# The second bias of the dense experts: one product of gates and biases for all token blocks, in place of a selector product per expert and block

## The chip, the core and the metric

The kernel runs on one core of one Trainium2 chip, in one launch. The metric is the device time of that core in microseconds (us). TensorE (PE) multiplies matrices, VectorE (DVE), ScalarE (ACT) and GpSimd (POOL) do the elementwise work, and SyncE (SP) issues the transfers. Each engine takes its own instructions in order and waits on semaphores for the others.

## What is computed

A two-layer language-model tower over 16 x 256 = 4096 tokens of width 256. Layer 0 has a time mix and a channel mix, then a mixture of 8 dense experts of width 1024. Layer 1 has a recurrence, attention with 16 heads, and 4 further experts. The change touches the 8 dense experts alone:

```python
logits = xf @ Wr + br                               # [tokens, 8]
weights = softmax(where(logits >= 2nd largest, logits, -inf))
h = gelu(einsum('td,edh->eth', xf, W1) + b1[:, None, :])
expert_out = einsum('eth,ehd->etd', h, W2) + b2[:, None, :]
out = einsum('etd,te->td', expert_out, weights)
```

`b2` is the second bias, one row of 256 numbers per expert. Its share of `out` is `weights @ b2`, a product of [4096 x 8] and [8 x 256].

## The kernel before, in words

The tokens are split into 8 blocks (TILES) of 512, each of 4 sub-blocks (SUB) of 128 tokens. `phase_a` (to about 520 us) makes layer 0 up to the input of the experts, for all blocks; the residual `c.h` stays in on-chip memory as fp32. `phase_bc` then runs passes. Pass i (0 to 7) takes the 8 dense experts of block i; from pass 1 on the layer-1 work of block i - 1 ("front": recurrence, attention, router) is woven in, and from pass 2 on the layer-1 experts of block i - 2 as well. Passes 3 to 6 are one loop. Two more passes hold the rest of layer 1. **Pass 0** (about 520 to 726 us) has dense work alone, and brings in and splits all weights (`low` on DVE, `high` on ACT). Passes 1 and 7 have dense and front work; passes 2 to 6 all three kinds.

All products are of bf16 parts: a fp32 number is a high and a low bf16 part, and a product takes three matmuls (high x high, low weight x high, high weight x low).

A pass of dense work is made of 64 units U0 to U63 ("up", 6 matmuls of 512 columns into one of two banks `c_up`) and 64 units D0 to D63 ("down", 12 matmuls of 256 columns into the two banks `c_down`). D8e to D8e+7 belong to expert e. ACT makes gelu of each U twice (fp32 `c_g` and bf16 `c_hi`), POOL makes the low part `c_lo`. D waits for both. After an expert's last D, DVE (`taken`, L1910) adds gate x `c_down` to `c.h`: four instructions.

In what order the units stand among the front's steps is written down in ORDER_F, which `Plan.braid` mixes with the plan's units by estimated costs; ORDER_0 is pass 0. Every engine goes through the same list and does its own part of each entry. In passes 2 to 6 the list near the dense units named later reads (front's steps by name, experts' units left out):

- `f1 U2 f1x U3 D0 U4 f2`: f1 transposes the normed input (L2004), f1x splits it (ACT, then POOL's `c_xlo`), f2 multiplies it (L1973).
- `Zx0 A1 U13 D8 D9 Z0 Rx1 ...`: the recurrence (A, R, Z steps), mostly DVE.
- `f5d U20 D16 D17 g5 U21 D18 f6`: f5d and g5 norm again (DVE, POOL), f6 transposes (L2004).
- `D24`, `D32`: among the heads of the first sequence (Sa, Sb score on PE, E the exponentials on ACT).
- `m3 D40 m4 D41 m5`: row maxima of the second sequence (PE scores into four banks, DVE reduces).
- `G20 D48 Sa6 E6`: among its heads, next to a gated expert unit.
- `g13 b0 U61 D56 D57 D58 U62 y0 D59 b1`: b0 and y0 norm (DVE, POOL), b1 transposes (L2004).

The bias before: `c.b2s` holds the three bf16 parts of `b2` for 8 experts in 24 of 128 rows, and `c.sel[:, e, :]` is a matrix of zeros with ones in the three rows of expert e. At the first D of an expert (D0, D8, ..., D56), each of the 4 sub-blocks starts with one matmul `c.sel[:, e, :] x c.b2s` (L2234), which puts the expert's bias row into every token's accumulator; the gate is applied later with the rest. These are 4 matmuls per expert and block, called "the selector group of D8e" below: 4 x 8 x 8 = 256.

Of the kernel before, what the change touches and what calls it, by code (L numbers as in the profile page):

```python
# [8 lines left out]
ALU = mybir.AluOpType  # L9
# [115 lines left out]
def phase_a(nc, c):  # L125
# [6 lines left out]
    with ExitStack() as x:  # L132
# [81 lines left out]
        def _(sp):  # L214
# [11 lines left out]
            for j in range(3):  # L226
                sp.wait_ge(s_p, 9 + 2 * j)
                sp.dma_start(c.b2s[j:3 * E0:3, :], c.b2p[:, j, :]).then_inc(s_b2, 16)
# [6 lines left out]
            sp.wait_ge(s_b2, 3 * 16)  # L235
# [739 lines left out]
def phase_bc(nc, c, out):  # L975


    KF, KE, KR = 109, 17, TILES * SUB + 5 + 13 + 2 * sum(kind != "B" for kind, _ in FIRST_LOADS)
    PB = GROUP
    VW = HD + 1  # L980
    with ExitStack() as x:
# [81 lines left out]
        w0 = mix0[:, :, :].rearrange("p s e -> p (s e)")  # L1063
        spare = lo14[:, 0:4, :].rearrange("p k n -> p (k n)").bitcast(F32)
# [35 lines left out]
        stored = count("stored", 16)  # L1100

# [71 lines left out]
        def run(eng, start, splits, dense, front, gates):  # L1173
# [3 lines left out]
            go(ORDER_0, splits, dense(0, PLAN_B, None))  # L1177
# [136 lines left out]
        def _(pool):  # L1314
# [69 lines left out]
            run(pool, lambda: None, {}, dense, front, lambda t: {})  # L1384

        @block.scalar
        def _(act):
# [163 lines left out]
            run(act, start, {"x%d" % u: lambda a=a: high(*a) for u, a in SPLITS.items()}, dense, front, gates)  # L1551

        @block.vector
        def _(dve):
# [407 lines left out]
            run(dve, start, {"x%d" % u: lambda a=a: low(*a) for u, a in SPLITS.items()}, dense, front, gates)  # L1962

        @block.tensor
        def _(pe):
# [220 lines left out]
            def dense(i, plan, before):  # L2186
# [37 lines left out]
                def down(u):  # L2224
# [78 lines left out]
            run(pe, lambda: None, {}, dense, front, lambda t: {})  # L2303
# [99 lines left out]
```

## Time and profile before

| | |
|---|---|
| times of three runs | 3225.17, 3230.91, 3234.37 us; median 3230.91 us |
| profiled execution | 3222.42 us, its span 3220.4 us |
| mean granted clock of TensorE | 0.959 of full speed |
| PE, ACT, DVE, POOL busy | 86%, 55%, 53%, 44% of the span |

The span is what the trace covers; 2.0 us of the execution lie around it. PE is the busiest engine, and what it waits for is spread thinly over the passes: how much a removed matmul is worth depends on what PE waits for next. In rows of the trace a matmul's duration includes the part in which it overlaps the next one, so the distance from one start to the next tells what one costs in a stream.

### The profile page before, as it was taken

The page shows a single profiled execution, that of the slowest core. Times are in us where ns is not written, and L with a number is a line of the kernel's source. Part 1 is how long each engine was busy: PE and PEld are TensorE (multiplying, and loading weights), DVE is VectorE, ACT ScalarE, POOL GpSimd, SP SyncE. Part 2 cuts the span into 40 slices and gives each one's busy share as a digit, 9 for nine tenths or more (in the row PEclk, how much of TensorE's full clock was granted, in tenths as well). Part 3 has the DMA queues.
Part 4 walks back from the last instruction along what each step waited for, and adds up shares of the span by engine and source line. Part 5 has one row for each costly group of instructions (what it writes and reads, how often), then busy time and mean ns, then how long its engine had stood idle before and what let it go on. Part 6 is the DMA issues. An engine that isn't in the chain of part 4 may idle for free. (4 is left out here: it accounts for less than half of the span.)

```text
span 3220.4 us, 58240 instructions
## 1 busy us (share of the span) xinstructions
PE 2778.5 (86%) x21884; PEld 1859.2 (58%) x22208; DVE 1695.8 (53%) x3163; ACT 1785.4 (55%) x2819; POOL 1407.7 (44%) x1326
## 2 busy tenths in 40 slices
PE   3787866898899999999999999999999998987778
PEld 1454544565665566566655665566656665663555
DVE  6777754636444635463446344635464446446552
ACT  2444534555665566656655665566556655664634
POOL 5454522443445444544454444444544343453334
PEclk8898987999999999999999999999999999999999
DMA  2000004842112122222222222222222222110002
GB/s 67 14 13 26 13 14 165 322 171 71 66 67 78 69 71 76 91 73 72 72 91 70 72 76 80 81 71 76 79 83 71 70 73 73 53 53 27 24 22 74
DMA packets 59721, 235.94 MB, mean 73 GB/s; under 512 B 6560, under 2 KB 25024, under 8 KB 40640
## 3 DMA queue, kind: packets, MB, share of 16 engines
q1 hardware_dynamic: 57920, 228.13, 20.3%
q0 software_dynamic: 1536, 4.20, 0.5%
q8 instruction: 176, 2.88, 0.4%
q14 instruction: 89, 0.73, 0.1%
HBM read 200.57 MB, written 31.72 MB: 72 GB/s over the span
## 5 line engine op out<-in xcount | busy, mean ns | idle before, releaser
L1381 POOL TENSOR_TENSOR c_lo<-c_g,c_hi 128x512 bf16<-128x512 f32 x720 | 888.2, 1241 | 1341.8 <-ACT c_hi L1543 1216.9
L2220 PE MATMUL c_up<-c_xT,c_ring 128*128 128x512 bf16 x2855 | 707.4, 384 | 78.4 <-ACT c_hi L1543 52.4
L2237 PE MATMUL c_down<-c_ring,c_hi 128*128 128x256 bf16 x4096 | 714.7, 275 | 0.0
L1542 ACT ACTIVATE c_g<-c_up,b 128x512 f32<-128x512 f32 x512 | 353.2, 690 | 491.5 <-PE c_up L2220 487.7
L2237 PE MATMUL c_down<-c_ring,c_lo 128*128 128x256 bf16 x2048 | 563.2, 275 | 0.0
L2220 PEld LDWEIGHTS c_up<-c_xT,c_ring 128*128 128x128 bf16 x3072 | 294.7, 99 | 362.3 <-ACT c_hi L1543 64.1
L2237 PEld LDWEIGHTS c_down<-c_ring,c_hi 128*128 128x128 bf16 x4096 | 397.4, 98 | 106.2 <-issue 1.7
L1543 ACT ACTIVATE c_hi<-c_up,b 128x512 bf16<-128x512 f32 x512 | 351.1, 686 | 0.0
L1809 DVE CAST c_room<-c_room 128x384 bf16<-128x384 f32 x256 | 127.1, 528 | 403.2 <-PE c_front L2132 307.8
L1542 ACT ACTIVATE c_g<-c_up 128x512 f32<-128x512 f32 x176 | 105.5, 600 | 291.7 <-PE c_up L1973 285.6
L2237 PEld LDWEIGHTS c_down<-c_ring,c_lo 128*128 128x128 bf16 x2048 | 201.5, 98 | 25.4
L1359 POOL TENSOR_TENSOR c_room<-c_room 128x384 bf16<-128x384 f32 x176 | 169.6, 977 | 61.4 <-DVE c_room L1809 61.4
L1973 PE MATMUL c_up<-c_hi,c_ring 128*128 128x512 bf16 x674 | 171.8, 388 | 19.7 <-ACT c_hi L1543 14.3
L2293 PE MATMUL c_down<-c_ring,c_hi 128*128 128x192 bf16 x1024 | 143.2, 258 | 25.0 <-DVE h L1910 25.0
L1973 PE MATMUL c_up<-c_yhi,c_ring 128*128 128x512 bf16 x476 | 131.4, 397 | 38.6 <-ACT c_hi L1543 26.2
L1910 DVE SCALAR_TENSOR_TENSOR h<-c_down,c_gates,h 128x256 f32<-128x256 f32 (+1 forms) x256 | 106.0, 475 | 81.9 <-PE c_down L2237 81.4
L1498 ACT ACTIVATE c_room<-c_front 128x384 f32<-128x384 f32 x256 | 115.7, 489 | 51.6 <-PE c_front L2108 47.4
L1784 DVE TENSOR_REDUCE c_mx<-c_front 128x2 f32<-128x512 f32 (+1 forms) x192 | 117.8, 682 | 47.4 <-PE c_front L2083 41.5
L1542 ACT ACT_TABLE_LOAD x101 | 129.6, 1283 | 10.9 <-PE c_up L2220 9.3
L2104 PE MATMUL c_front<-c_room,c_kz 128*128 128x256 bf16 (+1 forms) x512 | 120.0, 247 | 18.0 <-ACT c_room L1498 18.0
L2293 PE MATMUL c_down<-c_ring,c_lo 128*128 128x192 bf16 x512 | 132.0, 258 | 0.0
L1973 PEld LDWEIGHTS c_up<-c_hi,c_ring 128*128 128x128 bf16 x712 | 68.4, 99 | 90.6 <-issue 18.7
(334 smaller groups left out, 5439.2 us busy)
## 6 DMA issues: line engine op xcount, KB each, us to landing
c_ring<-kept_dense SPq DMA_DIRECT2D x112, 1024.0 KB, 4.8
c_ring<-kept_experts SPq DMA_DIRECT2D x63, 512.0 KB, 3.3
c_room<-in_WB SPq DMA_DIRECT2D x16, 1024.0 KB, 7.1
kept_dense<-c_ring SPq DMA_DIRECT2D x16, 1024.0 KB, 4.8
c_ring<-kept_experts SPq DMA_DIRECT2D x28, 384.0 KB, 3.4
kept_experts<-c_room SPq DMA_DIRECT2D x9, 512.0 KB, 4.1
c_xT<-kept_xT SPq DMA_DIRECT2D x8, 512.0 KB, 4.7
out<-h SPq DMA_DIRECT2D x8, 512.0 KB, 6.5
```

Source lines behind the costliest of these rows:

```text
L1359: pool.tensor_tensor(pl[:, n % PB, :], pf[:, n % PB, :], ph[:, n % PB, :], ALU.subtract).then_inc(p_lo_pool.sem, 1)
L1381: pool.tensor_tensor(lo14[:, a, :], g[:, h % 4, :], hi14[:, a, :], ALU.subtract).then_inc(lo_ready.sem, 1)
L1498: act.activation(pf[:, n % PB, :], fb[n % 2][:, 0:3 * P], ACT.Exp).then_inc(p_f.sem, 1)
L1542: act.activation(g[:, h % 4, :], ub[n % 2][:, :], ACT.Gelu, bias=bias)
L1543: act.activation(hi14[:, a, :], ub[n % 2][:, :], ACT.Gelu, bias=bias).then_inc(hi_ready.sem, 1)
L1784: dve.tensor_reduce(o, fb[n % 4][:, :].rearrange("p (h k) -> p h k", k=w), AX.X, ALU.max).then_inc(mx_ready.sem, 1)
L1809: dve.tensor_copy(ph[:, n % PB, :], pf[:, n % PB, :]).then_inc(p_hi.sem, 1)
L1973: m = pe.matmul(bank[:, :], w(wp, k, e * P, P), xs[xp][:, k, :], start=(j == 0 and k == 0), stop=(j == 2 and k == kc - 1))
L2104: pe.matmul(bank[:, lo:lo + w], kz[h % 2][:, h // 2, ks_:ks_ + P], qT[:, h // 2, qs_:SEQ], start=True, stop=False, skip_group_check=True)
L2220: last = pe.matmul(ub[n % 2][:, :], r[:, wp, o + q * P:o + (q + 1) * P], xT[:, xp, q, :], start=(m == 0 and q == 0), stop=(m == 2 and q == ...
L2237: m = pe.matmul(bank, (hi14, lo14)[xp][:, a, s * P:(s + 1) * P], r[:, wp, o + KC * P:o + CHUNK], start=False, stop=(k == HC0 - 1 and n == ...
L2293: m = pe.matmul(ob[s // 2][:, (s % 2) * D:(s % 2) * D + DZ], (hi14, lo14)[xp][:, a, s * P:(s + 1) * P], E(plan, wp, name, k, 0, DZ), start ...
```

## The change

The bias part is computed once for all 4096 tokens, in the second half of pass 0.

- DVE (`gate_parts`) clears 128 columns per sub-block in `lo14` (name `c_lo`), splits the fp32 gates into three bf16 parts, and writes six column groups of 8: BIAS lists which part of the gate meets which part of the bias (six of the nine pairs). `c.b2s` gets six groups of 8 rows to match (six small DMAs in place of three).
- PE transposes these 32 tiles of 128 x 128 in four rounds (gT0 to gT3) into the front's banks; ACT copies each round of 1024 columns to `hi14` (name `c_hi`).
- PE then makes 16 products of a pair of sub-blocks (`bias0` to `bias15`, two matmuls of 256 columns each), and DVE adds each (128 x 512) to `c.h`.
- ORDER_0 places them: gate parts behind D43, gT0 to gT3 behind D44 to D47, bias0 to bias15 behind D48 to D63.
- The 256 selector matmuls go. The first product of the group (L2280 in the changed kernel) starts the accumulation.

```diff
+BIAS = ((0, 0), (0, 1), (1, 0), (0, 2), (2, 0), (1, 1))
...
-            for j in range(3):
+            for m, (_, j) in sorted(enumerate(BIAS), key=lambda q: q[1][1]):
                 sp.wait_ge(s_p, 9 + 2 * j)
-                sp.dma_start(c.b2s[j:3 * E0:3, :], c.b2p[:, j, :]).then_inc(s_b2, 16)
+                sp.dma_start(c.b2s[m * E0:(m + 1) * E0, :], c.b2p[:, j, :]).then_inc(s_b2, 16)
...
+        bias = ["gparts"] + ["gT%d" % r for r in range(4)] + ["bias%d" % q for q in range(TILES * SUB // 2)]
         for u in PLAN_B.units:
             if u[0] == "U":
                 ORDER_0.append("x%d" % u[1])
             ORDER_0.append(u)
+            if u[0] == "D" and u[1] >= NB - len(bias):
+                ORDER_0.append(bias[u[1] - NB + len(bias)])
...
+            def transposed_gates(r):                      # ACT
+                def f():
+                    act.wait_ge(gT_ps.sem, r + 1)
+                    act.activation(gT[:, r * 8 * P:(r + 1) * 8 * P], fb[r][:, :].bitcast(BF16),
+                                   ACT.Copy).then_inc(gT_ready.sem, 1)
...
+            def gate_parts():                             # DVE
+                part = [gparts[:, :, m * E0:(m + 1) * E0] for m in range(len(BIAS))]
+                low_of = sl[:, 0:TILES * SUB * E0].rearrange("p (s e) -> p s e", e=E0)
+                R.done(dve.memset(lo14[:, 0:8, :], 0.0))
+                R.done(dve.tensor_copy(part[0], mix0[:, :, :]))
+                R.done(dve.tensor_tensor(low_of, mix0[:, :, :], part[0], ALU.subtract))
+                R.done(dve.tensor_copy(part[1], part[0]))
+                R.done(dve.tensor_copy(part[3], part[0]))
+                R.done(dve.tensor_copy(part[2], low_of))
+                R.done(dve.tensor_tensor(low_of, low_of, part[2], ALU.subtract))
+                R.done(dve.tensor_copy(part[5], part[2]))
+                R.done(dve.tensor_copy(part[4], low_of))
+            def bias(q):
+                def f():
+                    dve.wait_ge(bias_ps.sem, q + 1)
+                    at = slice(q * TT, (q + 1) * TT)
+                    dve.tensor_tensor(c.h[:, at], c.h[:, at], fb[q % 4][:, :], ALU.add).then_inc(bias_used.sem, 1)
...
-                            pe.matmul(bank, c.sel[:, e, :], c.b2s[:, :], start=(s % 2 == 0), stop=False,
-                                      skip_group_check=True)
                         for n, (wp, xp) in enumerate(PARTS):
                             m = pe.matmul(bank, (hi14, lo14)[xp][:, a, s * P:(s + 1) * P],
-                                          r[:, wp, o + KC * P:o + CHUNK], start=False, stop=(k == HC0 - 1 and n == 2),
+                                          r[:, wp, o + KC * P:o + CHUNK], start=(k == 0 and n == 0 and s % 2 == 0),
+                                          stop=(k == HC0 - 1 and n == 2),
...
+            def transposed_gates(r):                      # PE
+                def f():
+                    if r == 0:
+                        pe.wait_ge(r_steps.sem, r_steps.at(0, KR))
+                    for j in range(8):
+                        m = pe.transpose(fb[r][:, :].bitcast(BF16)[:, j * P:(j + 1) * P], gparts[:, 8 * r + j, :],
+                                         c.identb[:, :])
+                    m.then_inc(gT_ps.sem, 1)
+            def bias(q):
+                def f():
+                    pe.wait_ge(gT_ready.sem, q // 4 + 1 if q > 3 else 4)
+                    if q >= 4:
+                        pe.wait_ge(bias_used.sem, q - 3)
+                    for j in range(2):
+                        s = 2 * q + j
+                        m = pe.matmul(fb[q % 4][:, j * D:(j + 1) * D], gT[:, s * P:(s + 1) * P], c.b2s[:, :],
+                                      start=(j == 0), stop=True, skip_group_check=True)
+                    m.then_inc(bias_ps.sem, 1)
```

(In `gate_parts` the waits between dependent steps are left out here.)

PE's rows at the first D of the fifth expert of pass 0 (D40), before the change (buffer numbers shown, `c_down0` and `c_down1` are the two accumulators):

```order
L2220 MATMUL c_up0<-c_xT,c_ring3 128x512 x6
L2234 MATMUL c_down0<-b2s,sel 128x256
L2237 MATMUL c_down0<-c_ring2,c_hi14 128x256 x2
L2237 MATMUL c_down0<-c_ring2,c_lo14 128x256
L2234 MATMUL c_down0<-b2s,sel 128x256
L2237 MATMUL c_down0<-c_ring2,c_hi14 128x256 x2
L2237 MATMUL c_down0<-c_ring2,c_lo14 128x256
L2234 MATMUL c_down1<-b2s,sel 128x256
```

The L2234 rows go from every such place, and the rest stays in its order. PE's rows in pass 0 from the last quarter of D44 on, in the changed kernel (L2352 are the transposes of gT0, L2265 an up unit):

```order
L2280 MATMUL c_down1<-c_ring3,c_hi14 128x256 x2
L2280 MATMUL c_down1<-c_ring3,c_lo14 128x256
L2352 MATMUL c_front0<-identb,c_lo14 128x128 x8
L2265 MATMUL c_up0<-c_xT,c_ring0 128x512 x6
L2280 MATMUL c_down0<-c_ring3,c_hi14 128x256 x2
```

Eight transposes now stand between D44 and U48, and so on for three more units; behind each of the last sixteen D units stand two matmuls of 256 columns. DVE's rows in pass 0 around D43, in the changed kernel (L1613 is a split of arriving weights, L1983 to L1996 are the gate parts):

```order
L1926 SCALAR_TENSOR_TENSOR h<-c_down1,c_gates,h 128x256 x2
L1613 TENSOR_TENSOR c_ring1<-c_room0,c_ring1 128x1024 x2
L1983 MEMSET c_lo14 128x2048
L1985 CAST c_lo14<-c_gates 128x32x8
L1987 TENSOR_TENSOR c_sl<-c_gates,c_lo14 128x256
L1988 COPY c_lo14<-c_lo14 128x32x8
L1989 COPY c_lo14<-c_lo14 128x32x8
L1991 CAST c_lo14<-c_sl 128x32x8
L1993 TENSOR_TENSOR c_sl<-c_sl,c_lo14 128x256
```

The gate parts stand between the split of the weights that U52 to U55 use (L1613, `c_ring1`) and the next split, at U48's place in the list. Nothing else moves, but what stands behind them on DVE waits for them.

## Rows read from the trace of the kernel before

**Rows 1.** The page's busy time of each engine.

```profile
PE 2778.5 (86%) x21884; PEld 1859.2 (58%) x22208; DVE 1695.8 (53%) x3163; ACT 1785.4 (55%) x2819; POOL 1407.7 (44%) x1326
```

**Rows 2.** Groups by line and shape: busy us, mean ns; idle before, releasers.

```profile
L2234 PE MATMUL c_down<-b2s,sel 128*128 128x256 bf16 x256 | 71.2, 278 | 10.3 <-DVE h L1910 9.1 <-issue 1.1
```

**Rows 3.** Timeline of PE at D0 of pass 4: start us, us.

```profile
1661.23 0.27 PE L2234 MATMUL c_down<-b2s,sel 128*128 128x256 bf16 x1
1661.34 0.38 PE L2237 MATMUL c_down<-c_ring,c_hi 128*128 128x256 bf16 x2
```

**Rows 4.** Chain that ended last, pass 7: start us, us, what.

```profile
2618.43 0.27 PE c_down L2234
...
2655.62 3.36 DVE c_room L1702
...
2753.46 0.12 PE c_down L2234
...
2825.02 0.11 PE c_down L2234
...
2858.29 0.11 PE c_down L2234
```

**Rows 5.** Timeline of POOL and PE behind D0 of pass 4.

```profile
1662.95 2.27 POOL L1349 TENSOR_TENSOR c_xlo<-c_room,c_xhi 128x512 bf16<-128x512 f32 x2
...
1665.28 0.60 PE L1973 MATMUL c_front<-c_xlo,c_WF 128*128 128x512 bf16 x2
```

**Rows 6.** Timeline of PE behind D8, D40 and D48 of pass 4.

```profile
1717.75 0.59 PE L2220 MATMUL c_up<-c_xT,c_ring 128*128 128x512 bf16 x2 [0.87 <-ACT c_hi L1543]
...
1874.80 0.22 PE L2083 MATMUL c_front<-mask,identb 128*128 128x128 bf16 x1
1875.11 0.28 PE L2081 MATMUL c_front<-c_kz,c_room 128*128 128x256 bf16 x1
...
1910.70 0.28 PE L2104 MATMUL c_front<-c_room,c_kz 128*128 128x256 bf16 x1 [1.34 <-ACT c_room L1498]
```

**Rows 7.** PE's waits in pass 3 (1343 to 1662): us in total, times, longest.

```profile
PE c_down L2293 <- DVE h L1910: 4.8, 1, 4.8
...
PE c_front L2004 <- DVE c_xn L1572: 0.2, 1, 0.2
```

**Rows 8.** Timeline of ACT behind D24 of pass 4.

```profile
1813.86 0.93 ACT L1498 ACTIVATE c_room<-c_front 128x384 f32<-128x384 f32 x2 [0.48 <-PE c_front L2108]
```

**Rows 9.** Timeline of DVE and PE behind D56 of pass 4.

```profile
1952.02 2.03 DVE L1572 TENSOR_SCALAR c_xn<-c_h,c_brs 128x256 f32<-128x256 f32 x4 [1.73 <-POOL c_brs L1328]
...
1954.33 0.93 PE L2004 MATMUL c_front<-ident,c_xn 128*128 128x128 f32 x7
```

**Rows 10.** Pass 0's last part: stretch, us, busy of PE, PEld, DVE, ACT, POOL, granted clock, DMA.

```profile
655.00:726.00 71.00, 70.58 (x498) 49.17 (x504) 15.63 (x22) 40.00 (x60) 30.05 (x26) 1.00 0.47 173
```

**Rows 11.** Nearest rows for the new work, groups and one timeline row.

```profile
L1625 DVE MEMSET c_kz<- 64x1024 uint32 x2 | 1.8, 912 | 0.5 <-issue 0.5
L1764 DVE CAST c_qs<-c_room 128x256 bf16<-128x256 f32 x32 | 9.4, 294 | 2.2
L1721 DVE TENSOR_TENSOR h<-h,c_front 128x512 f32 x8 | 5.1, 679 | 0.0
L1477 ACT ACTIVATE c_room<-c_front 128x1024 bf16<-128x1024 bf16 x32 | 32.7, 1021 | 9.4 <-PE c_front L2063 9.4
1767.40 0.62 PE L2063 MATMUL c_front<-identb,c_ks 128*128 128x128 bf16 x8 [0.60 <-DVE c_ks L1771]
```

**Rows 12.** Timeline of DVE in pass 0, the split for U48.

```profile
680.97 1.27 DVE L1597 TENSOR_TENSOR c_ring<-c_room,c_ring 128x1024 bf16<-128x1024 f32 x1 [7.49 <-ACT c_ring L1406]
```

**Rows 13.** Timeline of DVE and PE where pass 1 begins.

```profile
730.90 4.73 DVE L1572 TENSOR_SCALAR c_xn<-h,c_fmv,c_frs 128x256 f32<-128x256 f32 x4 [1.40 <-POOL c_frs L1328]
...
736.44 1.04 PE L2004 MATMUL c_front<-ident,c_xn 128*128 128x128 f32 x8
```

**Rows 14.** Pass 4 behind the longest wait, columns as in rows 10.

```profile
1695.00:1698.40 3.40, 3.35 (x22) 3.04 (x23) 3.40 (x3) 0.00 (x0) 0.00 (x0) 0.52 0.00 0
```

More of the change, by code:

```diff
@@ L975, in phase_bc @@
 def phase_bc(nc, c, out):
-    KF, KE, KR = 109, 17, TILES * SUB + 5 + 13 + 2 * sum(kind != "B" for kind, _ in FIRST_LOADS)
+    KF, KE, KR = 109, 17, TILES * SUB + 5 + 13 + 9 + 2 * sum(kind != "B" for kind, _ in FIRST_LOADS)
     PB = GROUP
@@ L1063, in phase_bc @@
         w0 = mix0[:, :, :].rearrange("p s e -> p (s e)")
+        gparts = lo14[:, 0:8, :].rearrange("p k n -> p (k n)").rearrange("p (s r) -> p s r", r=P)
+        gT = hi14[:, 0:8, :].rearrange("p k n -> p (k n)")
         spare = lo14[:, 0:4, :].rearrange("p k n -> p (k n)").bitcast(F32)
@@ L1100, in phase_bc @@
         stored = count("stored", 16)
+        gT_ps, gT_ready, bias_ps, bias_used = (count(n, 0) for n in ("gT_ps", "gT_ready", "bias_ps", "bias_used"))
         up_ps = Both(x.enter_context(nc.semaphore("c_up_ps")), NB, len(PLAN_C.bank_user))
@@ L1171, in go, with run @@
                         stage[o]()
-        def run(eng, start, splits, dense, front, gates):
+        def run(eng, start, splits, biases, dense, front, gates):
             start()
-            go(ORDER_0, splits, dense(0, PLAN_B, None))
+            go(ORDER_0, splits, dense(0, PLAN_B, None), biases)
             go(ORDER_B, dense(1, PLAN_B, PLAN_B), front(0))
@@ L1383, in dense @@
                 return tokens_of(i, plan, step)
-            run(pool, lambda: None, {}, dense, front, lambda t: {})
+            run(pool, lambda: None, {}, {}, dense, front, lambda t: {})
         @block.scalar
@@ L1550, in gates @@
                 return {"r2x": r2x}
-            run(act, start, {"x%d" % u: lambda a=a: high(*a) for u, a in SPLITS.items()}, dense, front, gates)
+            def transposed_gates(r):
[3 more added lines that the diff above has]
+                                   ACT.Copy).then_inc(gT_ready.sem, 1)
+                return f
+            run(act, start, {"x%d" % u: lambda a=a: high(*a) for u, a in SPLITS.items()},
+                {"gT%d" % r: transposed_gates(r) for r in range(4)}, dense, front, gates)
         @block.vector
@@ L1961, in gates @@
                 return {"r2": r2}
-            run(dve, start, {"x%d" % u: lambda a=a: low(*a) for u, a in SPLITS.items()}, dense, front, gates)
+            def gate_parts():
+                part = [gparts[:, :, m * E0:(m + 1) * E0] for m in range(len(BIAS))]
+                low_of = sl[:, 0:TILES * SUB * E0].rearrange("p (s e) -> p s e", e=E0)
+                R.done(dve.memset(lo14[:, 0:8, :], 0.0))
+                R.settle()
+                R.done(dve.tensor_copy(part[0], mix0[:, :, :]))
+                R.settle()
+                R.done(dve.tensor_tensor(low_of, mix0[:, :, :], part[0], ALU.subtract))
+                R.done(dve.tensor_copy(part[1], part[0]))
+                R.done(dve.tensor_copy(part[3], part[0]))
+                R.settle()
+                R.done(dve.tensor_copy(part[2], low_of))
+                R.settle()
+                R.done(dve.tensor_tensor(low_of, low_of, part[2], ALU.subtract))
+                R.done(dve.tensor_copy(part[5], part[2]))
+                R.settle()
+                R.done(dve.tensor_copy(part[4], low_of))
+                assert R.n == KR
+            def bias(q):
[3 more added lines that the diff above has]
+                    dve.tensor_tensor(c.h[:, at], c.h[:, at], fb[q % 4][:, :], ALU.add).then_inc(bias_used.sem, 1)
+                return f
+            run(dve, start, {"x%d" % u: lambda a=a: low(*a) for u, a in SPLITS.items()},
+                {"gparts": gate_parts, **{"bias%d" % q: bias(q) for q in range(TILES * SUB // 2)}},
+                dense, front, gates)
         @block.tensor
@@ L2302, in dense @@
                 return tokens_of(i, plan, step)
-            run(pe, lambda: None, {}, dense, front, lambda t: {})
+            def transposed_gates(r):
[6 more added lines that the diff above has]
+                    m.then_inc(gT_ps.sem, 1)
+                return f
+            def bias(q):
[8 more added lines that the diff above has]
+                    m.then_inc(bias_ps.sem, 1)
+                return f
+            run(pe, lambda: None, {}, {**{"gT%d" % r: transposed_gates(r) for r in range(4)},
+                                       **{"bias%d" % q: bias(q) for q in range(TILES * SUB // 2)}},
+                dense, front, lambda t: {})
 def program(nc, ins, out):
```

2 lines of the change are left out of this document (1 added, 1 removed).

## The prediction

> **What bounds the kernel now.** I first read the page's busy time: PE works for 2778.5 of 3220.4 us [rows 1], so at first sight every matmul that goes is a gain. The groups by shape give the removed ones: 256 selector matmuls, 278 ns each by their rows [rows 2]. That mean is not what they cost. In PE's timeline the selector starts at 1661.23 and the next matmul at 1661.34 [rows 3]: the rest of the 0.27 us overlaps. A 256-column matmul in a stream costs 0.11 us, a selector group of four 0.44 us, all 64 groups 28.2 us.
>
> Whether the 0.44 us reaches the end depends on what PE meets next. If its next wait ends at a time that the earlier part of PE's queue does not set, the wait grows by 0.44 us and nothing is gained. So I read the chain that ended last (which can be followed through pass 7), the list of PE's waits in pass 3, and the timelines of PE, ACT, DVE and POOL behind each group of pass 4, which is like passes 2 to 6.
>
> In pass 7 the chain runs through the groups of D0, D32, D48 and D56 [rows 4]. Not so at D8 and D16, where it is on DVE for the recurrence (the reciprocal of 3.36 us is one piece), nor at D24 and D40. Pass 1 has the same list and I take the same four.
>
> In passes 2 to 6, group by group:
> - D0: the low part of f2 starts at 1665.28, and POOL ends `c_xlo` at 1662.95 + 2.27 = 1665.22 [rows 5]. PE already waits there, for work that began with f1 and U2, ahead of D0. Lost.
> - D8: the next wait is 0.87 us, for a gelu that stands on ACT behind exponentials for the recurrence [rows 6]. Lost. D16: f6 waits 0.2 us for DVE's norm [rows 7]. Lost.
> - D24: PE's next wait is for a gelu behind the exponentials of a head, and these had idled 0.48 us for PE's score matmuls [rows 8]. PE sets the chain. Kept; D32 likewise, four heads on.
> - D40: between m3 and m4 the score matmuls wait for DVE to free a bank, 0.31 us from one start to the next at 1874.80 where 0.06 us is a 128-column one's pace [rows 6]. Lost. D48: the next score waits 1.34 us for ACT, which is behind the gated unit started before D48 [rows 6]. Lost.
> - D56: DVE ends the norm at 1952.02 + 2.03 = 1954.05, and PE starts b1 at 1954.33 [rows 9]. Less the 0.06 us that the hand-over took at D0 [rows 5], some 0.2 us of the 0.44 can be kept.
>
> **The change, part by part.** *Removed in passes 1 and 7:* 2 x 4 x 0.44 = 3.5 us. *In passes 2 to 6:* 5 x (0.44 + 0.44 + 0.2) = 5.4 us. *In pass 0:* from 655 to 726 us PE is busy for 70.58 of 71.00 us at full clock [rows 10], and the groups of D32 (just before it), D40, D48 and D56 count: 1.8 us. The first four stand before waits for arriving weights, seen in the timeline, and are lost. Together 10.7 us.
>
> *Added on PE, all in that full stretch of pass 0.* 16 x 2 products of 256 columns at 0.11 us: 3.5 us. 32 transposes: eight of the same shape take 0.62 us with the overlap of the last [rows 11]. Less that overlap it is about 0.06 us each, with it 0.08; I take 0.06, the pace of a 128-column matmul: 1.9 us. Together 5.4 us, and nothing covers them.
>
> The Trainium skill (TensorE: Matmul & The Clock Gate, section Back-to-back issue gap) gives about 81 ns for each matmul of 128 columns in a stream of weight loads and matmuls. By it the transposes would cost 2.6 us and the sum below would be 0.7 us less of a gain. The eight transposes of rows 11 speak for the smaller figure.
>
> *Added on DVE: the gate parts.* Memset of 2048 words: twice the 1024 of 0.91 us, 1.8 us. Six copies or casts of 256 columns at 0.29 us, 1.8 us. Two subtractions of 256 columns, each under the 0.68 us for 512 columns, say 0.4 us [rows 11]. With the waits between them 4.6 us. DVE had been idle for 7.49 us before the split at 680.97 [rows 12], so they run from 673.5 to 678.1. PE comes to gT0 when D44 ends: 19 D and 16 U units of 12 x 0.11 = 1.3 us and two selector groups ahead of 726.3, about 679.9, and 0.9 us earlier for the two groups gone, 679.0. No wait, with 0.9 us to spare. Should DVE's steps take twice as long beside POOL, they end at 682.7 and PE stands 3.7 us: that is the upper bound. Behind them the split for U56 to U59 comes at most that much later, and it is needed some 20 us on.
>
> *ACT's four copies* of 1024 columns cost 1.02 us each [rows 11], 4.1 us, in a stretch where ACT is busy for 40 of 71 us. A late gelu holds an up unit only if it is two units late, and a unit takes PE 3.1 us here: hidden. *DVE's 16 additions* cost 0.68 us each [rows 11], under 15.6 of 71 us busy: hidden but for the last. It stands ahead of the norm of pass 1. The norm ends at 730.90 + 4.73 = 735.63 and PE starts f1 at 736.44 [rows 13], 0.8 us to spare. The addition takes 0.7 of it, and PE is there 0.2 us earlier (0.44 less for D0, 0.22 more for bias15). f1 then waits about 0.2 us, and I take that off D0 of pass 1. *PE waits for DVE* to free one of four banks only four products back, over 10 us. *SP's three more DMAs* of 8 rows are issued before the first pass of layer 0 has anything for SP: nothing.
>
> **The sum.** 10.7 - 0.2 - 5.4 = 5.1 us less: 3222.4 - 5.1 = 3217.3 us for the profiled execution. The median of the runs shown is 8.5 us above that execution, so the median after is 3230.9 - 5.1 = 3225.8, say 3226 us. Of the 28 us of PE's work that go, 5.4 come back in pass 0 and 17.5 vanish into waits that are there anyway.
>
> **The rivals.**
> *More of it lands.* The waits behind D0, D16, D48 end with engines that had themselves waited for PE not long before, so they could move along with it; a group's gain need not be all or nothing. If every group of passes 1 to 7 counts: 56 x 0.44 + 1.8 - 5.4 = 21.0 us less, 3210 us; half of the lost ones, some 13 us less, 3218 us. For it: PE's 86%. Against: the five waits above are seen in the rows, each begun by work ahead of the group. Chance 0.22 for a gain over 9.7 us.
> *Pass 0 pays and the rest gives nothing.* The groups kept run into a second wait just behind the first (0.48 us of ACT's idle time is only 0.04 more than a group), and PE stands for the gate parts. Nothing kept outside pass 0 gives 3.6 us more, and with the full wait of 3.7 us 7.3 us more: 3234 to 3238 us. This is slower from the point where under 8 of the 56 groups land. Chance 0.10.
> *The longer waits slow PE's clock.* Behind the longest wait of pass 4, 4.8 us [rows 7], PE ran for 3.4 us at a granted clock of 0.52 [rows 14], the lower level of 1.2 GHz, and lost 1.6 us. Each absorbed group makes a wait 0.44 us longer. If two more waits of each of the seven passes end this way, 14 x 1.6 = 22 us go against 5: 3248 us. It decides from three or four such events. Against: the waits that grow are now of 0.1 to 1.3 us. The same page of the Trainium skill (Part 1) says that an idle TensorE falls back to 1.2 GHz; rows 14 agree for a wait of 4.8 us. Chance 0.06.
>
> **How the numbers follow.** My own case, a gain of 0 to 9.7 us, has 0.62. A measurement of this kernel can tell about 0.3% from no change, 9.7 us. Faster by more than that: 0.22 from the first rival, and 0.02 from my own case by scatter. Slower by more: 0.04, from the clock rival. The same: 0.72. The range: the change from 14 us less to 6 us more holds all but 2 in 10, and about the median the runs scatter by -5.7 and +3.5 us. I take 3213 to 3237 us.
>
> **What would show it.** PE has 256 rows fewer of its selector, 32 transposes of about 0.06 us from start to start and 32 products of 0.11 us, and the D63 of pass 0 ends about 3.6 us later. Each of passes 2 to 6 is 1.1 us shorter, not 3.5. The waits of f2's low part (about 0.5 us), of f6, of the up unit behind D8 and of the score behind D48 are 0.4 us longer each. The gate parts end before PE asks for them. I am wrong if the passes shorten by over 2 us each, if PE waits over 1 us for the gate parts, or if a stretch of low clock appears that was not there.

## The result and the profile after

| | before | changed |
|---|---|---|
| median of the runs | 3234.4 us (20 runs, 3225.2 to 3239.1) | 3244.9 us (20 runs, 3231.3 to 3251.0) |
| profiled execution | 3222.4 us | 3251.0 us |
| mean granted clock, profiled | 0.959 | 0.953 |

The ratio is 1.0030 (95%: 1.0022 to 1.0039): the change costs about 10 us where I forecast a gain of 5, and the time lies outside my range. The two profiled executions stand at opposite ends of their runs. Of their difference of 28.6 us some 18 are scatter, so a reading of the two traces alone overstates everything; what follows is read as "where", and "how much" is left to the experiments.

What should have gone is gone, and what was added costs what it should. The page of the changed kernel, busy time of each engine (as in [rows 1]):

```profile
PE 2798.9 (86%) x22016; PEld 1845.2 (57%) x22016; DVE 1701.5 (52%) x3188; ACT 1790.3 (55%) x2823; POOL 1406.6 (43%) x1326
```

PE's busy time is no evidence here: before has 21884 matmuls beside 22208 weight loads [rows 1], so 324 records are missing, and the changed kernel has all 22016. The lines of the transposes and the products in the changed kernel: duration min/median/max in ns, first and last start:

```profile
L2352 PE MATMUL c_front<-identb,c_lo x32: 219/219/219, 681.6 to 691.1; 128*128 128x128 bf16 x32
its engine sat idle before it (us, times) until:
...
L2364 PE MATMUL c_front<-b2s,c_hi x32: 272/273/273, 695.1 to 732.3; 128*128 128x256 bf16 x32
its engine sat idle before it (us, times) until:
```

Nothing stands behind "idle before": PE never waited for them. So where does it wait? PE's waits over the whole span (total, times, longest), before and changed:

```profile
PE c_up L2220 <- ACT c_hi L1543: 52.4, 34, 4.2
...
PE c_front L2004 <- DVE c_xn L1572: 18.2, 10, 3.7
...
PE c_up L1973 <- issue: 8.8, 6, 2.8
```

```profile
PE c_up L2265 <- ACT c_hi L1552: 58.7, 40, 4.2
...
PE c_front L2049 <- DVE c_xn L1588: 25.0, 11, 3.7
...
PE c_up L2018 <- issue: 12.2, 6, 3.2
```

Two waits grew and will matter: 3.4 us of "issue" in front of layer-1 expert units, where PE waited for nothing that the profile shows, and 6.8 us in front of transposes of the normed input. (The waits for gelus in front of dense up units grew by 6.3 us too, but this sum scatters: it is 51.6 us in after_pe_half_packet, which has the change as well, and 54.2 in before_again, which is the kernel before.) A third is in DVE's timeline at D48 of pass 4, before and changed:

```profile
1902.24 0.63 DVE L1809 CAST c_room<-c_room 128x384 bf16<-128x384 f32 x2 [11.46 <-PE c_front L2132]
```

```profile
1915.25 1.61 DVE L1825 CAST c_room<-c_room 128x384 bf16<-128x384 f32 x2 [11.83 <-PE c_front L2177]
1916.90 1.15 DVE L1828 TENSOR_TENSOR c_room<-c_room 128x384 bf16<-128x384 f32 x1
1917.97 1.65 DVE L1926 SCALAR_TENSOR_TENSOR h<-c_down,c_gates,h 128x256 f32 x4
```

POOL at the same place, before and changed:

```profile
1902.58 1.30 POOL L1381 TENSOR_TENSOR c_lo<-c_g,c_hi 128x512 bf16<-128x512 f32 x1 [3.96 <-ACT c_hi L1543]
```

```profile
1915.22 1.16 POOL L1390 TENSOR_TENSOR c_lo<-c_g,c_hi 128x512 bf16<-128x512 f32 x1 [3.96 <-ACT c_hi L1552]
```

DVE starts its two casts 0.37 us later behind the same release (11.83 for 11.46 us). They now start behind POOL's subtraction, where they had started ahead of it. They take 1.61 for 0.63 us, and the `taken` of the fifth expert behind them holds D48. PE's row there in the changed kernel:

```profile
1918.89 0.39 PE L2280 MATMUL c_down<-c_ring,c_hi 128*128 128x256 bf16 x2 [0.83 <-DVE h L1926]
```

It is the same in each of passes 3 to 6 and in none outside the loop: 4 x 0.83 = 3.3 us of waiting. And PE behind the loop's branch from pass 4 to 5, before, then changed:

```profile
1966.26 0.81 PE L1973 MATMUL c_up<-c_yhi,c_ring 128*128 128x512 bf16 x3 [2.74 <-issue]
```

```profile
1979.70 1.63 PE L2018 MATMUL c_up<-c_yhi,c_ring 128*128 128x512 bf16 x4 [2.84 <-issue]
1981.13 1.06 PE L2018 MATMUL c_up<-c_ylo,c_ring 128*128 128x512 bf16 x2
1981.98 0.63 PE L2018 MATMUL c_up<-c_yhi,c_ring 128*128 128x512 bf16 x1
1983.35 1.46 PE L2018 MATMUL c_up<-c_yhi,c_ring 128*128 128x512 bf16 x3 [0.73 <-issue]
```

A second gap stands in the unit behind the first, and the matmuls run at half pace. The windows of the same stretch, before and changed, and of passes 4 to 6 (columns as in [rows 10]):

```profile
1963.50:1973.70 10.20, 7.46 (x35) 3.18 (x36) 4.52 (x16) 5.38 (x9) 1.95 (x3) 1.00 0.35 126
...
1660.00:2620.00 960.00, 884.36 (x7272) 601.77 (x7381) 482.10 (x897) 568.71 (x895) 432.59 (x393) 0.99 0.22 76
```

```profile
1976.59:1986.80 10.21, 6.63 (x19) 2.07 (x17) 4.32 (x17) 2.17 (x4) 1.56 (x3) 0.67 0.29 106
...
1662.00:2640.00 978.00, 898.25 (x7288) 598.12 (x7289) 471.06 (x879) 568.59 (x897) 434.62 (x393) 0.97 0.21 74
```

The clock is granted at 1.00 before and 0.67 after, that is partly at the lower level of 1.2 GHz. So low stretches appeared, as my third rival said, but one of them behind the loop's branch, where no removed group stands. What this place and D48's share is that an engine is late for no reason but its stream of instructions. The page of the changed kernel has that stream as transfers:

```profile
q8 instruction: 178, 2.92, 0.4%
q14 instruction: 90, 0.74, 0.1%
```

Instructions come in packets of 2.92 MB / 178 = 16.4 KB and 0.74 / 90 = 8.2 KB. With 58224 instructions in the trace that is 63 bytes each, an estimate, and so some 256 and 128 in a packet. PE's weight loads and matmuls alone are 44032 of the 58224, so the larger packets must be PE's. The Trainium skill (Runtime: NRT & Kernel Launch, section Instruction fetch mechanics) states blocks of 256 instructions for the refill, and a stall where a branch leaves the pages at hand. The larger packet and PE's 2.74 us behind the branch agree; the smaller packet of 8.2 KB is not in it.

**Theories.** A: the waits that absorb a group grow and PE's clock falls behind them (my rival). B: chance of the one execution. C: the work in pass 0 costs more than 5.4 us. D: the change shifts the code of the loop in its packets (DVE's by 25 instructions, PE's by 52 fewer: 192 of the selector gone from passes 0 to 2, 140 added), and delays that hang on where a packet begins fall where they hurt.

### The profile page after: what moved, and what is told of

Read it like the earlier page. It is cut to its first block and busy times, and to the rows that moved or that the text cites. A ratio compares the mean times of both kernels' runs of the same rounds, so it can differ in the third digit from the quotient of the medians.

```text
span 3249.2 us, 58224 instructions
## 1 busy us (share of the span) xinstructions
PE 2798.9 (86%) x22016; PEld 1845.2 (57%) x22016; DVE 1701.5 (52%) x3188; ACT 1790.3 (55%) x2823; POOL 1406.6 (43%) x1326
## 3 DMA queue, kind: packets, MB, share of 16 engines
q8 instruction: 178, 2.92, 0.4%
## 5 line engine op out<-in xcount | busy, mean ns | idle before, releaser
L2265 PE MATMUL c_up<-c_xT,c_ring 128*128 128x512 bf16 x3072 | 751.9, 384 | 72.5 <-ACT c_hi L1552 58.7
L2280 PE MATMUL c_down<-c_ring,c_hi 128*128 128x256 bf16 x4096 | 706.6, 275 | 11.4 <-DVE h L1926 9.8
L2280 PE MATMUL c_down<-c_ring,c_lo 128*128 128x256 bf16 x2048 | 563.3, 275 | 0.0
L2265 PEld LDWEIGHTS c_up<-c_xT,c_ring 128*128 128x128 bf16 x3072 | 295.5, 99 | 371.1 <-ACT c_hi L1552 69.1
L2280 PEld LDWEIGHTS c_down<-c_ring,c_hi 128*128 128x128 bf16 x4096 | 395.8, 99 | 127.2 <-issue 11.0
L2280 PEld LDWEIGHTS c_down<-c_ring,c_lo 128*128 128x128 bf16 x2048 | 202.3, 99 | 25.1
L2018 PE MATMUL c_up<-c_yhi,c_ring 128*128 128x512 bf16 x504 | 144.4, 412 | 41.1 <-ACT c_hi L1552 26.3
```

Source lines behind the costliest of these rows:

```text
L2018: m = pe.matmul(bank[:, :], w(wp, k, e * P, P), xs[xp][:, k, :], start=(j == 0 and k == 0), stop=(j == 2 and k == kc - 1))
L2265: last = pe.matmul(ub[n % 2][:, :], r[:, wp, o + q * P:o + (q + 1) * P], xT[:, xp, q, :], start=(m == 0 and q == 0), stop=(m == 2 and q == ...
```

## The experiments

Each ratio is to runs of the kernel before on the same chip; 0.1% is 3.2 us.

**One half of the change at a time.** `removal_only` deletes the selector matmul from the kernel before, `addition_only` and `selector_at_lost` put it back into the changed kernel, in all groups or in 35 of them. `before_again` is the kernel before. (removal_only has no second bias at all; the other two add bias rows that don't belong to the sum.)

```diff
# removal_only
-                            pe.matmul(bank, c.sel[:, e, :], c.b2s[:, :], start=(s % 2 == 0), stop=False, ...
# selector_at_lost (addition_only: without the condition)
+                            if before is not None and e in (0, 1, 2, 5, 6):
+                                pe.matmul(bank, c.sel[:, e, :], c.b2s[:, :], start=(s % 2 == 0), stop=False, ...
```

> The kernel before, unchanged, to learn how its granted clock and its low stretches differ from one execution to the next. In its shown profile 6 steps at the low clock stand between 1660 and 2620 us, in the changed kernel 17. Theory A (the grown waits slow the clock): this kernel shows about 6 again and a mean clock near 0.959. Theory B (chance of the one execution): the count of this kernel varies as widely, up to the 17 of the changed one, and the mean clock of its runs lies between 0.953 and 0.959.

> The kernel before without the 256 selector matmuls; the second bias of the dense experts is left out altogether. Theory A (grown waits slow the clock, 10 us or more): no faster than before, 3233 to 3240 us, with a mean clock at least 0.003 lower. Theory C (the removal gives what was predicted, 10.7 us, and the work added in pass 0 costs 20 us instead of 5): 3223 to 3225 us, clock as before.

> The changed kernel with all 256 selector matmuls put back as well (they add rows of the bias that do not belong to the sum, so the output is not the reference's). Theory A: the waits are as long as before and only pass 0 is longer, by the 4 to 6 us that its trace shows: 3238 to 3241 us, clock as before. Theory C: 3250 to 3256 us. Theory D (the instructions added ahead of the loop shift its code and so lengthen the gaps without a releaser at the loop's boundary): 3243 to 3250 us, with gaps of over 0.6 us in the second unit behind the boundary, as the changed kernel shows.

> The changed kernel with the selector matmuls put back in passes 1 to 7 at D0, D8, D16, D40 and D48, the places where I took their 0.44 us for absorbed (35 groups; their rows add a part of the bias that does not belong to the sum). If absorbed work is worth nothing by itself and only the clock pays for its absence (theory A): 3 to 10 us faster than the changed kernel, 3235 to 3242 us, clock at least 0.001 higher. If the groups counted after all (the first rival): up to 15 us slower, 3250 to 3260 us. If neither: 3245 us and the same clock.

Measured: 3220.6, 3215.4, 3235.0 and 3222.8 us where before has 3219.8; ratios 1.0007 (0.9997 to 1.0016), 0.9982 (0.9970 to 0.9994), 1.0045 (1.0032 to 1.0058), 1.0007 (0.9998 to 1.0016). B holds in part: before_again has a mean clock of 0.956 to 0.961 in its runs, and 10 low steps in its trace where the shown one has 6. The removal gains, and the addition costs 14 us (5 runs of it only) though it has every selector of before: A falls as the main cause. What points to D and not C is in the traces: in all three kernels with DVE's new instructions, the cast at D48 starts 0.4 us late in every iteration, and in none of the others.

**The code moved, and nothing else.** DVE gets one-column memsets and PE matmuls of 4 columns, at the start of pass 0, where DVE idles some 3 us and PE some 9.

```diff
+                for n in range(25):                          # DVE; 103, 128 in others
+                    dve.memset(pad[:, n:n + 1], 0.0)
                 low(0, 0)
+            def pe_pads():                                   # PE; 26, 58, 90, 96, 114, 128 in others
+                for n in range(102):
+                    pe.matmul(fb[0][:, 4 * n:4 * n + 4], c.identb[:, :], c.identb[:, 0:4], start=True, stop=True, ...
```

> The kernel before with 25 one-column memsets on DVE at the start of pass 0 (under 1 us of DVE's idle time), nothing else. Theory D: the gap of 0.40 us and the wait of D48 appear in passes 3 to 6 (4 x 0.83 = 3.3 us), and the kernel is 3 to 6 us slower than before. Theory A, and every theory in which the work itself counts: no change, within 1 us of before.

> The kernel before with 102 matmuls of 4 columns on PE at the start of pass 0 (2.7 us of its 8.7 us of idle time there). The 204 instructions and the change's 52 fewer differ by 256, about one packet of 16.4 KB, so PE's loop starts where it does in the changed kernel, and nothing else is changed. Theory D for PE: three more gaps of 0.73 us without a releaser, 3 to 8 us slower than before. If only DVE's place counts: within 1.5 us of before.

> The kernel before with 128 memsets on DVE and 128 matmuls of 4 columns (256 instructions) on PE at the start of pass 0: more instructions than in either kernel that got 9 us slower (25 on DVE; 204 on PE), but by about one whole packet of each engine, so that the loop's code stands at the same place in its packets. Theory D (the place in the packet decides): within 0.15% of before, cast at D48 behind a gap of 0.04 us, at most 6 gaps without a releaser ahead of layer-1 expert units. If the number of added instructions or their own time is what costs: 9 us slower or more.

| kernel | memsets, matmuls added | ratio to before | "issue" in front of layer-1 units: us, times |
|---|---|---|---|
| before_again | 0, 0 | 1.0007 (0.9997 to 1.0016) | 8.0, 3 |
| before_dve_code_moved | 25, 0 | 1.0029 (1.0017 to 1.0042) | 10.1, 6 |
| before_pe_code_moved | 0, 102 | 1.0029 (1.0018 to 1.0039) | 14.9, 9 |
| before_whole_packet | 128, 128 | 1.0003 (0.9989 to 1.0017) | 7.8, 3 |

So 25 instructions on DVE that take under 1 us of its idle time cost the kernel before 9 us (5 to 14), 102 tiny matmuls on PE as much (6 to 13), and more of both, but a whole packet, nothing that can be measured (-4 to 5). It is neither the work of the pads nor their number, nor the tile that the memsets write, which before_whole_packet has too. DVE's rows at D48 of pass 4, in before_dve_code_moved and before_whole_packet:

```profile
1913.59 1.61 DVE L1812 CAST c_room<-c_room 128x384 bf16<-128x384 f32 x2 [11.83 <-PE c_front L2135]
1915.24 1.16 DVE L1815 TENSOR_TENSOR c_room<-c_room 128x384 bf16<-128x384 f32 x1
1916.31 1.65 DVE L1913 SCALAR_TENSOR_TENSOR h<-c_down,c_gates,h 128x256 f32 x4
```

```profile
1903.28 0.63 DVE L1812 CAST c_room<-c_room 128x384 bf16<-128x384 f32 x2 [11.46 <-PE c_front L2135]
```

And PE behind the loop's branch in before_pe_code_moved, where a second gap of 2.31 us now stands beside the first:

```profile
1968.36 0.81 PE L1973 MATMUL c_up<-c_yhi,c_ring 128*128 128x512 bf16 x3 [2.85 <-issue]
...
1972.13 0.82 PE L1973 MATMUL c_up<-c_yhi,c_ring 128*128 128x512 bf16 x3 [2.31 <-issue]
```

**Where the delays sit.** The traces of all 19 kernels have every instruction, also those that work on registers alone and are left out of the views. On DVE, the cast at D48 starts 0.42 us behind the instruction ahead of it in the five kernels in which DVE has 25 more instructions ahead of the loop than before, and 0.06 us in the other 14, in which it has as many as before or 128 more. In those 14 a register instruction that lies 25 further on in the loop starts 0.37 to 0.40 us behind the one ahead of it, and in the five 0.02. It is so in all four passes of the loop. The delay thus stays at one place of the code, and the instructions move across it by the 25 that were added; in the old place it falls where DVE is about to wait anyway. Behind it the next packet of 8.2 KB starts, 0.7 to 1.0 us later in the 14 kernels and 1.7 to 2.4 in the five.

On PE, the second gap ends at the same weight load in all four kernels that have one (the changed kernel, after_again, after_dve_code_moved, before_pe_code_moved), 7.9 to 8.3 us behind the branch, and the other 15 have none. Counted in instructions modulo 256, the loop lies 204 further than in the kernel before in the four, and 0, 28, 64, 128 or 140 further in the others. In every kernel a packet of 16.4 KB starts about 1 us behind the branch and lands at 1.9 to 2.8 us, and the next starts at 5.2 to 6.1 and lands at 6.2 to 7.0 us. That the second gap is PE waiting for this next packet, whose code it needs earlier in that one placement, fits all of this and is not shown directly: no view ties an instruction to its packet.

**The changed kernel with its code put back.** `after_again` is the changed kernel.

> The changed kernel, unchanged, on the chip of the three kernels below, with the granted clock of each run beside that of the kernel before. Theory A (absorbed groups slow the clock) and theory D (the place of the code decides) both expect 9 to 12 us more than before. The clock tells how much of it is PE at the low level: a mean clock 0.003 below that of before would be 0.003 x 3240 = 10 us, the whole of it; the same clock would leave 10 us of waits and work.

> The changed kernel with 103 one-column memsets on DVE at the start of pass 0, where DVE idles 3 us. In all three kernels with the 25 new DVE instructions a cast of the heads at D48 starts 0.40 us after its wait ended instead of 0.04 us, in each of passes 3 to 6, and in none of the three kernels without them. Instructions come in packets of 8.2 KB, at about 63 bytes each 128 to 130 of them; 25 + 103 = 128 puts DVE's code of the loop back to the same place in its packet. Theory D: the 0.40 us gap goes, the cast takes 0.36 again instead of 1.35 us, D48 no longer waits 0.83 us for DVE, and the kernel is 3.3 us or more faster than the changed one. Theory A: no effect, within 1 us of the changed kernel.

> The changed kernel with the 103 memsets on DVE and 26 matmuls of 4 columns on PE (52 instructions with their weight loads, the number by which PE's code ahead of the loop became shorter; about 1 us of PE's idle time at the start of pass 0). Theory D for both engines: the extra gaps of 0.73 us without a releaser behind the loop's boundary go too, 3 in the changed kernel's trace, and it is 2 to 5 us faster than the kernel with DVE's code moved alone. If PE's gaps don't come from where the loop starts in a packet: the same time as that kernel, within 1.5 us.

> The changed kernel with DVE's code moved back to its place (103 memsets) and PE's 128 instructions further than in the kernel with both in place (90 matmuls of 4 columns). Theory D: PE's gaps without a releaser depend on where the loop lies in its packets, so this is another time than the 3223 us of the kernel with both in place, by 3 us or more in either sense. If the kernel with both in place was faster for another reason: 3223 us again.

| kernel | memsets, matmuls added | ratio to before | "issue": us, times |
|---|---|---|---|
| after_again | 0, 0 | 1.0051 (1.0036 to 1.0067) | 15.2, 9 |
| after_dve_code_moved | 103, 0 | 1.0028 (1.0018 to 1.0038) | 15.1, 9 |
| after_both_moved | 103, 26 | 1.0006 (0.9996 to 1.0017) | 9.2, 6 |
| after_pe_half_packet | 103, 90 | 1.0000 (0.9985 to 1.0015) | 9.5, 7 |

DVE's place gives back some 7 us and PE's another 7, with DVE's idle time at D48 back at 11.46 us in the first, and the second gaps gone in the second. At half a packet PE's time is not measurably another: I expected 3 us or more. Not every distance costs, and the traces say why: of the six placements of PE's loop, 204 alone has the second gap.

**Each half with the code in place.** These repeat the two halves with pads (the removal with PE 96, the addition with DVE 103 and PE 58).

> The kernel before without the selector matmuls (the second bias left out), with 96 matmuls of 4 columns on PE at the start of pass 0 that fill up the 192 instructions by which PE's code ahead of the loop got shorter. With every engine's loop at its old place this is the removal by itself. My sum gave 10.7 us (range by its rivals 2 to 26). If the sum is right: 3208 to 3211 us where before has 3220. If absorbed groups cost something through the clock: under 7 us less, 3213 to 3218.

> The changed kernel with all selector matmuls put back (they add rows of the bias that do not belong to the sum), 103 memsets on DVE and 58 matmuls of 4 columns on PE, so that both engines' code of the loop stands where it did in its packets. Without them this cost 14 us. Theory D: most of that goes and what is left is the work in pass 0, 4 to 7 us: 3224 to 3227 us where before has 3220. If the work in pass 0 is what costs: still 3234.

Measured: 0.9975 (0.9962 to 0.9988), 8.1 us less, and 1.0021 (1.0010 to 1.0032), 6.8 us more, of 3229.1 us. Theory C is out: the addition is what it was priced at within its interval (3 to 10 us), and about half of its 14 us was the place of the code. That half was DVE's: addition_only has the delay at D48 and, with PE's loop 140 instructions further, no second gap.

**What the last microseconds are.**

> The changed kernel with the selector matmuls back at D0, D8, D16, D40 and D48 of passes 1 to 7 (they add a part of the bias that does not belong to the sum), and both engines' loop code in place (103 memsets, 114 matmuls of 4 columns). Against the kernel with both in place it has 35 groups more, 15.4 us of PE work. If the waits absorb them and nothing else: the same time within 1.5 us. If their absence lengthens waits behind which PE's clock falls (theory A): 2 to 5 us faster, with a higher mean clock. If they counted: up to 15 us slower.

> The changed kernel with DVE's and PE's code of the loop in place (103 memsets, 26 matmuls of 4 columns), and the list gparts, gT0 to gT3, bias0 to bias15 placed behind D14 to D34 of pass 0 in place of D43 to D63. There PE waits for arriving weights (in 560 to 590 us it is busy 24.6 of 30). If the addition costs PE's work in the full stretch, this hides it: 4 to 7 us faster than the kernel with both in place, so about 0.15% faster than the kernel before. If DVE's additions there hold up the splits of the weights instead: no gain, or up to 10 us slower.

> The kernel with both engines' code in place once more, for a direct comparison with the two above on one chip: within 0.15% of the kernel before, as the first time (1.0006).

> The changed kernel with the bias steps behind D14 to D34, DVE's code in place, and PE's code of the loop 64 instructions further (58 matmuls of 4 columns), the place that it has in the kernel with the removal alone, whose trace had only 3 such gaps of 7.8 us where those in place have 6 of 9.4. If these gaps are all that is left: 2 to 4 us faster than before. If the profile's count of small gaps says nothing: as the early version in place, 1.0003 of before.

Measured: 1.0000 (0.9987 to 1.0013), 1.0003 (0.9988 to 1.0018), 1.0006 (0.9993 to 1.0019), and 0.9989 (0.9980 to 0.9998) with 8.5 us in 3 gaps. The 35 absorbed groups are worth nothing measurable, in either sense: 2 us less with them than without (1.0000 for 1.0006), with some 6 us of scatter, where they are 15.4 us of PE's work. Moving the bias steps to where PE waits for weights, edited as

```diff
-            if u[0] == "D" and u[1] >= NB - len(bias):
-                ORDER_0.append(bias[u[1] - NB + len(bias)])
+            if u[0] == "D" and 14 <= u[1] < 14 + len(bias):
+                ORDER_0.append(bias[u[1] - 14])
```

gives 1 us (1.0003 for 1.0006) with some 6 us of scatter, so the 4 to 7 us that I expected are neither seen nor excluded. Only with PE's code at yet another place is a version of the change faster than before, by 3.5 us, and the upper end of that interval nearly touches no change; it is one of several places tried.

One result doesn't fit the 9 us of DVE's place. selector_at_lost has DVE's code where the changed kernel has it, with the same 0.83 us of PE's waiting at D48 in four passes, and is at 1.0007; lost_in_place, the same work with the code in place, is at 1.0000. That is 2 us with some 5 us of scatter. D48's wait accounts for 3.3 us. What the rest of the 9 us is, and whether it is there in every kernel, isn't settled.

## Why the prediction was wrong

**The step that failed: "Nothing else moves".** My front part says this of DVE's order, and my sum rests on the same thought: that of 256 removed, 64 added PE matmuls and 25 DVE instructions only their own time counts. In the order of the work it is true. But they move the code behind them in the packets in which instructions arrive, and that costs 9 us for DVE's shift alone, 9 for PE's, and for the changed kernel all but some 2 of its 10 us (1.0030; 1.0051 in the second measurement, whose interval overlaps the first). "10.7 - 0.2 - 5.4" has no term for it. With the code in place the changed kernel stands at 1.0006, twice: 2 us more (1 less to 5 more in the first, 2 less to 6 more in the second), where I had 5 less.

**A second step that failed: the 5.4 us of passes 2 to 6.** "Each of passes 2 to 6 is 1.1 us shorter" is not so in the loop. From the first weight load of one pass's dense work to that of the next, passes 3, 4 and 5 take 324.0, 324.2 and 324.2 us in the kernel before, 324.0, 324.5 and 324.0 in removal_only, and 324.0 each in after_both_moved; executions with more steps at the low clock have passes of 325 to 329 us with and without the selector. I called D24 "Kept". In the list of PE's waits of removal_only stands:

```profile
PE c_front L2104 <- ACT c_negT L1489: 1.3, 5, 0.3
```

This is a wait right behind D24, 0.2 to 0.3 us once in each of passes 2 to 6. Every kernel without the selector at D24 has it, and none that has the selector there. So D24's group was absorbed and not kept. The other loss is f6's, shown below. Counted from the loop's branch, in passes 4 and 6 of removal_only, PE is 0.7 us earlier than before behind D16, 0.6 us later behind f6, still 0.6 later behind D24's wait, 0.2 later behind D32, 0.1 later behind the waits of D40 and of D48, 0.3 earlier behind D56 and 0.05 earlier or less at the pass's end. D32 and D56 gave what I had kept, and f6 and D24 took it back.

**The removed groups, -10.7 us.** Measured -8.1 (-12 to -4). The sum is right within the interval, but by luck, since the loop's share of it (4 x 1.1 us) isn't there. Pass 1 gave at least its 1.8 us: it takes 281.8 and 281.3 us in the two kernels with the removal alone, for 283.0 to 285.4 in the five traces of before and before with pads. Where the rest comes from isn't settled: in these five, pass 0 takes 191 to 196 us and all from pass 7 on 606 to 611 us (190 and 193, and 609, without the selector). What f6 took in passes 2 to 6 begins at D8 and D16, which I had as worth nothing: their removal makes f6 later. Timelines of POOL, DVE and PE at f6 of pass 4, before and changed:

```profile
1741.61 2.31 POOL L1381 TENSOR_TENSOR c_lo<-c_g,c_hi 128x512 bf16<-128x512 f32 x2
1741.69 3.03 DVE L1572 TENSOR_SCALAR c_xn<-h,c_fmv,c_frs 128x256 f32 x4 [3.59 <-POOL c_frs L1343]
...
1744.75 1.31 POOL L1381 TENSOR_TENSOR c_lo<-c_g,c_hi 128x512 bf16<-128x512 f32 x1 [0.83 <-ACT c_hi L1543]
...
1744.78 1.09 PE L2004 MATMUL c_front<-ident,c_xn 128*128 128x128 f32 x8 [0.17 <-DVE c_xn L1572]
```

```profile
1752.64 2.32 POOL L1390 TENSOR_TENSOR c_lo<-c_g,c_hi 128x512 bf16<-128x512 f32 x2
1752.73 3.91 DVE L1588 TENSOR_SCALAR c_xn<-h,c_fmv,c_frs 128x256 f32 x4 [3.61 <-POOL c_frs L1352]
1755.34 1.15 POOL L1390 TENSOR_TENSOR c_lo<-c_g,c_hi 128x512 bf16<-128x512 f32 x1 [0.37 <-ACT c_hi L1552]
...
1756.69 0.55 PE L2049 MATMUL c_front<-ident,c_xn 128*128 128x128 f32 x3 [1.50 <-DVE c_xn L1588]
```

POOL's third low part starts 2.70 us behind the first two, where it was 3.14: PE comes to its up unit 0.44 us earlier. It now falls on the norm (`c_xn`) in place of what stands behind it. The norm takes 3.91 for 3.03 us, and f6 waits 1.50 for 0.17. I had said that this wait grows by 0.4; it grows by 1.3. From the end of the longest wait of each pass (the 4.8 us of [rows 7]) to f6 it is 49.6 to 49.7 us in passes 3 to 6 before and 50.2 or more in the changed kernel, so some 0.5 us are lost in each pass. The Trainium skill (SBUF — State Buffer, section Terms) has DVE and POOL share one pair of ports, exclusively for the length of an instruction. The trace agrees: with POOL's third subtraction on it the norm takes 3.91 us, without it 3.03, and the instructions behind it (`c_h`) shrink from 2.22 to 1.37 us in return. PE's waits for this norm sum to 25.0 us in the changed kernel and in removal_pe_in_place, and to 18.2 with the two groups in place (before, addition_both_in_place, lost_in_place).

**The added work, +5.4 us, and f1's wait, +0.2.** Right within the interval. PE starts the unit behind D63 at 732.45 for 726.59, 5.9 us later, of which 1.7 are there at the first unit of the pass (532.5 for 530.8): 4.2 where I had 3.6. f1 has no wait (the norm ends at 742.07, PE starts it at 742.45), since D0 ahead of it waits 0.50 for ACT. The eight transposes of gT0 take 0.61 us, the price of [rows 11]. The gate parts run from 676.10 to 681.09, 5.0 us where I had 4.6 (the second subtraction, which starts 0.09 us behind one of POOL's, takes 1.35 us where the first takes 0.42), and PE asks at 681.56: no wait, with 0.5 us to spare for my 0.9. ACT's copies and DVE's additions were hidden. That placing the work earlier gains nothing measurable leaves open whether anything but PE's own time is in the 6.8 us.

**D48's wait for ACT, 1.34 us in [rows 6], would be 0.4 longer.** With the code in place it is. In the changed kernel as it stands the new wait, D48's own for DVE, stands ahead of it.

**The rivals.** More landing (0.22): no; the absorbed 35 groups are worth nothing measurable. Pass 0 pays and the rest gives nothing (0.10): not as a whole, since the removal gives 8 us, but for the loop's passes it is what the traces show. The clock (0.06): the clock did fall, but by another way than I gave. With PE's code moved the mean granted clock of the kernel before, over its runs, fell from 0.9565 to 0.9537, where PE executes the same work. At the removed groups no such effect can be told from scatter (lost_in_place 0.9570, both_moved_again 0.9563, the runs of before beside them 0.9567). Nor do the gaps at the branch explain it alone: with the same second gap after_dve_code_moved has 0.9578 beside 0.9581, and a step at the low clock within 20 us behind the branch stands in 9 of 12 passes with a second gap and in 22 of 45 without. Of the cost, how much is the gap itself and how much the slow matmuls behind it isn't settled: the two overlap in the same microseconds.

The prediction doesn't speak of "issue" at all. The row that could have warned me is in the list of PE's waits of before: 8.8 us of it in front of layer-1 units, up to 2.8 at a time, behind the loop's branch.

## What to carry to other kernels

In a kernel with a loop and long straight code, an edit that changes how many instructions an engine has ahead of the loop is also a change of where the loop lies in its packets, here worth up to 9 us of 3230 for each of two engines, more than the edit. Before an effect of under 0.5% is put down to the work, run the same edit with the old number of instructions (or whole packets of harmless ones in the engines' idle time), and look at the waits on "issue" and at DVE's idle times to a hundredth of a microsecond. And work that a wait absorbs isn't free to take away: what comes earlier may land on another engine's ports.

## What had not been expected of the hardware

- One place in the straight code of the loop delays DVE by some 0.36 us (11.46 to 11.83 us of idle time at D48), in each iteration, and stays where it is when instructions are added ahead of the loop; on its own harmless, but two casts then start behind POOL's subtraction and take 1.61 us in place of 0.63. That it is a packet's end is inferred, from 128 added instructions that leave it as it was and from the packet that starts behind it.
- Behind the loop's branch PE stands 2.4 to 3.5 us in any placement, and in one of six another 0.2 to 2.3 us in the next unit.
- The granted clock differs from execution to execution of one kernel: 0.956 to 0.961 in the 12 runs of before_again, at 3215.5 to 3229.3 us.
